# Graph attention on one Trainium2 core: both products of one late unit in sixteen from PSUM, two loads' room given to second sigmoids

## The chip, the cores and the metric

The kernel runs on one core of one Trainium2 chip. The metric is the device time of one execution in microseconds (us), lower is better.

## The reference

Two layers over N = 8192 nodes with 128 features, a dense 8192x8192 matrix `adj`, all in float32.

```python
# layer 0
A' = alpha * adj, with (1 - alpha) added on the diagonal
x1 = layernorm(x + relu((A' @ x / rowsum(A')) @ W.T + b))
# layer 1
t    = logmap0(x1)                               # a factor for each row
par  = adj   * sigmoid(t @ w_par[:d] [:, None] + t @ w_par[d:] [None, :] + b_par)
chi  = adj.T * sigmoid(t @ w_chi[:d] [:, None] + t @ w_chi[d:] [None, :] + b_chi)
out  = layernorm(x1 + proj(expmap0(chi @ t + par @ t)))
```

Almost all of the work of layer 1 is elementwise on 8192x8192: for each element two sigmoids, two products with `adj` or its transpose, and a product with the 128 columns of `t` on TensorE.

## The kernel before

The nodes are cut into 8 panels of 1024 rows. **Layer 0** goes over 256 pairs of tiles (`pair(g)`): SyncE loads 128x2048 values of `adj`, TensorE multiplies them with `x`, VectorE sums degrees. **Layer 1** is cut into 512 units. A unit n is one output panel p (1024 rows) against one tile jt of 128 columns, so 128x1024 elements, and it takes these steps:

- ScalarE (`sigmoids`, lines 707 to 738) computes the second sigmoid `chi(n)` (line 720) into an SBUF buffer and the first one (line 737) into a PSUM slot.
- GpSimd (`second_product`, lines 533 to 538) multiplies `chi(n)` in place with the untransposed tile ("nat", DRAM name in_a_cols).
- VectorE (`first_product`, line 986) multiplies the PSUM slot in place with the transposed tile ("trn", in_g_blk), and (`key`, line 995) adds `chi(n)` to it into one of three SBUF buffers `keys(n)`.
- TensorE (`products`, line 1180) multiplies `keys(n)` with the tile of `t` and sums into `outp`.

A unit of the set `APART` (line 268: n % 8 == 2 from unit 194, 35 units) has no `key`: VectorE writes its first product to `keys(n)`, and TensorE multiplies `keys(n)` and then `chi(n)` (line 1186), which adds the two in PSUM. Its buffer of `chi` is free only when TensorE has read it.

Units 0 to 153 are strewn into layer 0. Units 154 to 511 are the **late** ones, which come behind it. The late units go panel by panel: 64 units of one panel and, from 34 units on, 8 of an early one, so a period of the plan is 72 units. The last 8 of the 64 are the panel's **own** tiles (units 224 to 231, 296 to 303, 368 to 375, 440 to 447, 504 to 511), for which no transposed tile is loaded: TensorE transposes it from the nat tiles into the PSUM slot (`turn_own`, line 1196), two units ahead, and ScalarE writes the first sigmoid to SBUF. All 8 units of an own block need a part of all 4 nat loads, so these 4 entries come free only when the last transpose is done (line 469).

The order of everything is written out by hand and each engine works through its own list. What matters around the change:

- **Loads.** SyncE issues 1 MB loads (line 513), nat then trn for each two units, in order, into a ring of 7 entries in `ring` and from unit 160 on 3 more in `xA` (`RING`, `EXTRA`, lines 34 and 35). `wait_free` (line 454) waits until the entry's last user is through: `m2_ready`, counted by GpSimd's products, for nat, and `m1_ready`, by VectorE's first products, for trn.
- **Second sigmoids.** `buffer_of` (line 259) gives three buffers, and four from `MORE` = unit 184 on, where the fourth is a part of `xA`. ScalarE writes `chi(n)` when unit n-4 has been added (`k_ready`), or, where n-4 is in `APART`, multiplied by TensorE (`kt_used`). The last part of `xA` is a buffer for the own blocks (line 341).
- **PSUM slots.** `slot_plan` (line 144) hands out slots in turn, three from `SLOT_THREE` = unit 202 on. ScalarE's first sigmoid of unit n waits until the slot's last holder is done (`slot_free`, line 432). The norms of a finished panel (line 1205, 6 units into the next) and its transposed output (line 1215, 18 units in) each take a slot in the same rotation.
- **Finished panels.** In between, `evacuate` (760), the norms and their root (776, with a change of ScalarE's activation table), GpSimd's small steps, `add_residual` (1014), statistics (1022) and `final_normalise` (793, one of eight parts before each of eight units) run for one panel 34 or 38 units after the last.

```python
if before in APART:
    act.wait_ge(kt_used, before + 1)
elif before is not None:
    act.wait_ge(k_ready, SUMS[before])
```

Of the kernel before, what the change touches and what calls it, by code (L numbers as in the profile page):

```python
# [13 lines left out]
BP = 1024  # L14
# [17 lines left out]
PAIRS = NPAN * PPP  # L32
EARLY = 3
RING = 7
EXTRA = 3
CB = 3
KB = 3
SB = 3
PE_LAG = 2
# [101 lines left out]
SLOT_TWO, SLOT_THREE = LATE0, LATE0 + 48  # L141


def slot_plan():

    plans = {"unit": {}, "norms": {}, "final": {}}
    holder = {0: ("layer 0", 0), 1: ("passage", 0), 2: None}
    starts = {b + F_NORMS_SLOT: ("norms", k) for k, (_, b) in enumerate(FINALS)}
    starts |= {b + F_SLOT: ("final", k) for k, (_, b) in enumerate(FINALS)}
    uses = []  # L150
    for n in range(UNITS):
        if n in starts:
            uses.append(starts[n] + (n,))
        uses.append(("unit", n, n))
    uses += [("norms", len(FINALS) - 1, UNITS), ("final", len(FINALS) - 1, UNITS)]
    last = 2
    for kind, i, n in uses:
        if n < SLOT_TWO:
            s = 2
        elif n < SLOT_THREE:  # L160
            s = 0 if last == 2 else 2
        else:
            s = (last + 1) % SB
        last = s
        plans[kind][i] = (s, holder[s])
        holder[s] = (kind, i)
    return plans["unit"], plans["norms"], plans["final"]


SLOT_OF_UNIT, SLOT_OF_NORMS, SLOT_OF_FINAL = slot_plan()  # L170


def load_plan():

    kinds = []
# [80 lines left out]
MORE = LATE0 + 30  # L256


def buffer_of(n, few):

    if n < MORE:
        return n % few, n - few if n >= few else None
    k = (n - MORE) % (few + 1)
    return (few, n - few - 1 if n > MORE else None) if k == 0 else ((MORE + k - 1) % few, n - few - 1)

APART = {n for n in range(MORE + 8, UNITS) if n % 8 == 2 and n not in OWN_AT}

SUMS = [n + 1 - sum(m in APART for m in range(n + 1)) for n in range(UNITS)]  # L270

# [6 lines left out]
def adj_resnorm_kernel(nc, x_g, xT, g_blk, a_blk, WT, b_row, alpha, w_par, b_par, w_chi, b_chi, out):  # L278
    with ExitStack() as ctx:
# [3 lines left out]
        def sem(name):  # L283
            return ctx.enter_context(nc.semaphore(name))
# [46 lines left out]

        def chi(n):

            b, _ = buffer_of(n, CB)
            return chi_few[:, b, :] if b < CB else xA[:, EXTRA * CH:EXTRA * CH + BP]

        def keys(n):
            return keys_few[:, n % KB, :]


        own_par = [taken[:, :], xA[:, EXTRA * CH + BP:EXTRA * CH + 2 * BP]]

        def natural_of_own(n, k):

# [2 lines left out]
        def loaded(kind, j):  # L347

            e, c = LOAD_OF[(kind, j)]
            return entry(e), r_in[e], 16 * c  # L350
# [57 lines left out]
        m1_ready = sem("m1_ready")  # L408
        m2_ready = sem("m2_ready")
        k_ready = sem("k_ready")  # L410
        kt_used = sem("kt_used")
        out_evac = sem("out_evac")
        acc_added = sem("acc_added")
# [19 lines left out]
        def slot_free(eng, before):  # L433

            kind, i = before
            if kind == "unit" and i in APART:
                eng.wait_ge(m1_ready, i + 1)
            elif kind == "unit":
                eng.wait_ge(k_ready, SUMS[i])
            elif kind == "norms":  # L440
                eng.wait_ge(f_norm, i + 1)
            elif kind == "final":
                eng.wait_ge(v_ready, i + 1)
            elif kind == "layer 0":
                eng.wait_ge(y_evac, NPAN)
            else:
                eng.wait_ge(rows_ready, NPAN)
                eng.wait_ge(prcr_ready, NPAN)
# [3 lines left out]
        @block.sync  # L452
        def _(sp):
            def wait_free(e, before):
                if before is None:
                    if e >= RING:
                        sp.wait_ge(l0_used, PAIRS)
                    return
                kind, j = before
                if kind == "pair":  # L460

                    sp.wait_ge(l0_used, j + 1)
                    sp.wait_ge(deg_added, j + 2 if j % PPP == 0 else j + 1)
                elif kind == "trn":
                    sp.wait_ge(m1_ready, 2 * j + 2)
                else:
                    sp.wait_ge(m2_ready, 2 * j + 2)
                    if 2 * j in OWN_AT:
                        sp.wait_ge(own_turned, (OWN_AT[2 * j] // TPP + 1) * TPP)

            def load_x1(k):
                p, _ = FINALS[k]
                if k < 2:
                    sp.wait_ge(x1_out, 16 * NPAN)
                    sp.wait_ge(xt_ready, NPAN)
# [12 lines left out]

            for kind, j, e, before, _ in LOADS:
                if kind == "pair":  # L490
                    r, q = divmod(j, PPP)
                    if r == 0 and q % 2 == 0:
                        G = q // 2
                        src = x_g[G].rearrange("(a t) (c s d) -> s a c t d", t=2, s=2, d=D)
                        for h in range(2):
                            for c in range(2):
                                at = G * GC + c * 2 * D
                                sp.dma_start(xA[h * P // 2:(h + 1) * P // 2, at:at + 2 * D]
                                             .rearrange("a (t d) -> a t d", t=2), src[h, :, c]).then_inc(x_in[G], 16)
# [12 lines left out]
                wait_free(e, before)  # L512
                sp.dma_start(entry(e), src.rearrange("(p t) c -> p (t c)", t=2)).then_inc(r_in[e], 16)
            load_x1(NPAN - 1)
            store(NPAN - 2)
            store(NPAN - 1)
            sp.wait_ge(out_done, 16 * NPAN)

        @block.gpsimd
        def _(pool):  # L520
# [10 lines left out]
                                   op=ALU.add).then_inc(folded, 1)  # L531

            def second_product(n):
                t, here, count = loaded("nat", n // 2)
                pool.wait_ge(here, count)
                pool.wait_ge(c_ready, n + 1)
                pool.tensor_tensor(out=chi(n), in0=chi(n), in1=half(t, n),  # L537
                                   op=ALU.mult).then_inc(m2_ready, 1)
# [74 lines left out]
        def _(act):  # L613
# [93 lines left out]
            def sigmoids(n):  # L707
# [1 line left out]
                row, c, _ = rows_of(n)  # L709
                act.wait_ge(l_in[row], 32 * c)  # L710
                act.wait_ge(prcr_ready, jt // TPP + 1)
                b, before = buffer_of(n, CB)
                if before in APART:
                    act.wait_ge(kt_used, before + 1)
                elif before is not None:
                    act.wait_ge(k_ready, SUMS[before])
                elif b == CB:
                    act.wait_ge(l0_used, PAIRS)
                    act.wait_ge(res_ready, NPAN)
                act.activation(chi(n), scores[:, row, 1, :], ACT.Sigmoid,  # L720
                               bias=prcr[:, 2 * jt + 1:2 * jt + 2]).then_inc(c_ready, 1)
                if n in OWN_AT:
                    i = OWN_AT[n]
# [140 lines left out]
        def _(dve):  # L864
# [109 lines left out]
            def first_product(n):  # L974
# [10 lines left out]
                    dve.wait_ge(kt_used, n - KB + 1)  # L985
                dve.tensor_tensor(out=keys(n) if n in APART else s, in0=s, in1=other, op=ALU.mult).then_inc(m1_ready, 1)  # L986

            def key(n):
                if n in APART:
                    return  # L990
                dve.wait_ge(m1_ready, n + 1)
                dve.wait_ge(m2_ready, n + 1)
                if n >= KB:
                    dve.wait_ge(kt_used, n - KB + 1)
                dve.tensor_tensor(out=keys(n), in0=slots[SLOT_OF_UNIT[n][0]], in1=chi(n),  # L995
# [80 lines left out]
            for n in range(N_EARLY, UNITS):  # L1076
# [3 lines left out]
                    final(k, n - b)  # L1080
                if n == N_EARLY and PAIRS - 1 in UNIT_AT:
                    key(n - 1)
                first_product(n)
                key(n)
            k = NPAN - 1
# [9 lines left out]
        def _(pe):  # L1095
# [65 lines left out]
            def products(n):  # L1161
# [19 lines left out]
                                    keys(n)[:, h * BANK:(h + 1) * BANK], start=begins,  # L1181
                                    stop=is_end(n) and n not in APART)
                if n in APART:
                    pe.wait_ge(m2_ready, n + 1)
                    for h in range(BP // BANK):
                        ins = pe.matmul(outp[:, h * BANK:(h + 1) * BANK], xtA[:, jt * D:(jt + 1) * D],  # L1186
                                        chi(n)[:, h * BANK:(h + 1) * BANK], start=False, stop=is_end(n))
# [86 lines left out]
```

## Time and profile before

| | |
|---|---|
| Time, median of 3 runs | 2234.77 us (2233.01 to 2239.25) |
| Time of the profiled execution | 2237.35 us |
| Its span, first to last instruction | 2235.5 us |
| TensorE busy | 2039.8 us (91%) |
| VectorE busy | 1935.9 us (87%) |
| ScalarE busy | 1326.9 us (59%) |
| GpSimd busy | 1334.1 us (60%) |
| Moved by DMA | 818.29 MB, mean 366 GB/s |
| Mean granted TensorE clock | 0.976 |

The shares are means over two very different parts: layer 0 up to about 1255 us, in which ScalarE and GpSimd do little, and the late units from there to about 2212 us. Names in the profile: `ps` is a PSUM slot or `outp`, `chi` and `xA` the buffers of second sigmoids (`xA` also ring entries), `ring` the loads, in_a_cols a nat load and in_g_blk a trn load. PE is TensorE, DVE VectorE, ACT ScalarE, POOL GpSimd, SP SyncE. DMA landing times and waits are as the profile infers them from semaphores.

### The profile page before, as it was taken

The page shows a single profiled execution, that of the slowest core. Times are in us where ns is not written, and L with a number is a line of the kernel's source. Part 1 is how long each engine was busy: PE and PEld are TensorE (multiplying, and loading weights), DVE is VectorE, ACT ScalarE, POOL GpSimd, SP SyncE. Part 2 cuts the span into 40 slices and gives each one's busy share as a digit, 9 for nine tenths or more (in the row PEclk, how much of TensorE's full clock was granted, in tenths as well). Part 3 has the DMA queues.
Part 4 walks back from the last instruction along what each step waited for, and adds up shares of the span by engine and source line. Part 5 has one row for each costly group of instructions (what it writes and reads, how often), then busy time and mean ns, then how long its engine had stood idle before and what let it go on. Part 6 is the DMA issues. An engine that isn't in the chain of part 4 may idle for free. (4 is left out here: it accounts for less than half of the span.)

```text
span 2235.5 us, 18654 instructions
## 1 busy us (share of the span) xinstructions
PE 2039.8 (91%) x5240; PEld 919.1 (41%) x5240; DVE 1935.9 (87%) x1854; ACT 1326.9 (59%) x1512; POOL 1334.1 (60%) x607
## 2 busy tenths in 40 slices
PE   8999999999999999999999976998888889889886
PEld 3344444444444434444444432343344334334334
DVE  4676878988989988998998988898998998989996
ACT  0011324454454454453453587889888989999996
POOL 0000305435455555643543676999998998999995
PEclk9999999999999999999999988999999999999998
DMA  9998989899889988888888998999999999998992
GB/s 313 333 343 300 387 299 365 361 366 381 361 347 403 405 344 358 347 357 338 369 356 316 421 421 317 384 363 421 421 393 403 421 420 376 421 421 347 421 421 97
DMA packets 129207, 818.29 MB, mean 366 GB/s; under 512 B 14912, under 2 KB 27456, under 8 KB 33360
## 3 DMA queue, kind: packets, MB, share of 16 engines
q1 hardware_dynamic: 122304, 796.97, 89.1%
q10 hardware_dynamic: 6800, 20.13, 2.5%
q8 instruction: 43, 0.70, 0.1%
q14 instruction: 60, 0.49, 0.1%
HBM read 808.59 MB, written 8.45 MB: 365 GB/s over the span
## 5 line engine op out<-in xcount | busy, mean ns | idle before, releaser
L537 POOL TENSOR_TENSOR chi<-chi,ring 128x1024 f32<-128x1024 f32 x323 | 826.9, 2573 | 662.7 <-ACT chi L720 603.5
L1180 PE MATMUL ps<-keys,xtA 128*128 128x512 f32 x2048 | 986.4, 615 | 135.4 <-DVE keys L995 106.1
L1108 PE MATMUL ps<-ring,xA 128*128 128x512 f32 x2048 | 922.5, 600 | 37.9 <-DMA ring<-in_g_blk 33.6
L737 ACT ACTIVATE ps<-scores,prcr 128x1024 f32<-128x1024 f32 x472 | 521.9, 1106 | 389.5 <-DVE keys L995 379.2
L1180 PEld LDWEIGHTS ps<-keys,xtA 128*128 128x128 f32 x2048 | 382.3, 195 | 668.1 <-issue 629.0
L888 DVE TENSOR_TENSOR dsum<-dsum,ring 128x2048 f32<-128x2048 f32 x240 | 593.2, 2472 | 44.7 <-DMA ring<-in_g_blk 37.4
L1108 PEld LDWEIGHTS ps<-ring,xA 128*128 128x128 f32 x2048 | 386.5, 192 | 533.3 <-issue 468.8
L995 DVE TENSOR_TENSOR keys<-ps,chi 128x1024 f32<-128x1024 f32 x395 | 483.7, 1224 | 78.2 <-issue 29.2
L986 DVE TENSOR_TENSOR ps<-ps,ring 128x1024 f32<-128x1024 f32 x381 | 465.9, 1223 | 74.2 <-ACT ps L737 71.1
L720 ACT ACTIVATE chi<-scores,prcr 128x1024 f32<-128x1024 f32 x430 | 488.7, 1137 | 61.0 <-PE ps L1186 45.8
L537 POOL TENSOR_TENSOR chi<-chi,xA 128x1024 f32<-128x1024 f32 x107 | 251.9, 2372 | 32.4 <-ACT chi L720 32.3
L537 POOL TENSOR_TENSOR xA<-xA,ring 128x1024 f32<-128x1024 f32 x49 | 116.2, 2372 | 1.6 <-ACT xA L720 1.6
L995 DVE TENSOR_TENSOR keys<-ps,xA 128x1024 f32<-128x1024 f32 x82 | 100.4, 1225 | 6.6 <-DVE ps L986 2.4
L986 DVE TENSOR_TENSOR ps<-ps,xA 128x1024 f32<-128x1024 f32 x76 | 93.0, 1224 | 14.4 <-ACT ps L737 12.9
L530 POOL TENSOR_TENSOR dsum<-dsum 128x1024 f32<-128x1024 f32 x8 | 18.8, 2354 | 139.6 <-DVE dsum L888 137.2
L720 ACT ACTIVATE xA<-scores,prcr 128x1024 f32<-128x1024 f32 x82 | 93.0, 1134 | 0.4 <-ACT yb L671 0.4
L630 ACT ACTIVATE small<-mv,epsc 128x8 f32<-128x8 f32 x8 | 2.4, 301 | 150.6 <-DVE mv L922 150.6
L537 POOL TENSOR_TENSOR xA<-xA 128x1024 f32<-128x1024 f32 x33 | 78.3, 2374 | 5.0 <-ACT xA L720 5.0
L1186 PE MATMUL ps<-chi,xtA 128*128 128x512 f32 x140 | 65.8, 592 | 0.0
L884 DVE TENSOR_TENSOR dsum<-ring 128x1024 f32<-128x1024 f32 x16 | 34.3, 2182 | 31.8 <-PE ps L1117 17.4
L546 POOL TENSOR_TENSOR acc<-taken,acc 128x1024 f32<-128x1024 f32 x15 | 37.4, 2490 | 31.0 <-ACT taken L753 31.0
L720 ACT ACT_TABLE_LOAD x28 | 35.9, 1283 | 26.8 <-DVE prcr L954 22.6
(109 smaller groups left out, 818.6 us busy)
## 6 DMA issues: line engine op xcount, KB each, us to landing
ring<-in_g_blk SPq DMA_DIRECT2D x461, 1024.0 KB, 10.0
ring<-in_a_cols SPq DMA_DIRECT2D x186, 1024.0 KB, 9.9
xA<-in_a_cols SPq DMA_DIRECT2D x70, 1024.0 KB, 10.9
xA<-in_g_blk SPq DMA_DIRECT2D x31, 1024.0 KB, 12.6
scores<-plcl_d ACTq DMA_DIRECT2D x22, 512.0 KB, 8.1
xA<-in_x_g SPq DMA_DIRECT2D x64, 64.0 KB, 13.4
yb<-in_xT ACTq DMA_DIRECT2D x8, 512.0 KB, 8.8
x_d<-res ACTq DMA_DIRECT2D x8, 512.0 KB, 8.5
```

The source lines that it names most:

```text
L530: pool.tensor_tensor(out=dsum[:, 0:BP], in0=dsum[:, 0:BP], in1=dsum[:, BP:2 * BP], op=ALU.add).then_inc(folded, 1)
L537: pool.tensor_tensor(out=chi(n), in0=chi(n), in1=half(t, n), op=ALU.mult).then_inc(m2_ready, 1)
L546: pool.tensor_tensor(out=at, in0=taken[:, :], in1=at, op=ALU.add).then_inc(acc_added, 1)
L720: act.activation(chi(n), scores[:, row, 1, :], ACT.Sigmoid, bias=prcr[:, 2 * jt + 1:2 * jt + 2]).then_inc(c_ready, 1)
L737: act.activation(dst, scores[:, row, 0, :], ACT.Sigmoid, bias=prcr[:, 2 * jt:2 * jt + 1]).then_inc(p_ready, 1)
L884: dve.tensor_tensor(out=half(dsum, h), in0=half(t0, h), in1=half(t, h), op=ALU.add) \
L888: dve.tensor_tensor(out=dsum[:, :], in0=dsum[:, :], in1=t, op=ALU.add).then_inc(deg_added, 1)
L986: dve.tensor_tensor(out=keys(n) if n in APART else s, in0=s, in1=other, op=ALU.mult).then_inc(m1_ready, 1)
L995: dve.tensor_tensor(out=keys(n), in0=slots[SLOT_OF_UNIT[n][0]], in1=chi(n), op=ALU.add).then_inc(k_ready, 1)
L1108: ins = pe.matmul(Y[:, h * BANK:(h + 1) * BANK], xA[:, tile * D:(tile + 1) * D], t[:, tt * BP + h * BANK:tt * BP + (h + 1) * BANK], start= ...
L1180: ins = pe.matmul(outp[:, h * BANK:(h + 1) * BANK], xtA[:, jt * D:(jt + 1) * D], keys(n)[:, h * BANK:(h + 1) * BANK], start=begins, stop=i ...
L1186: ins = pe.matmul(outp[:, h * BANK:(h + 1) * BANK], xtA[:, jt * D:(jt + 1) * D], chi(n)[:, h * BANK:(h + 1) * BANK], start=False, stop=is_ ...
```

## The change

Seventeen late units, those with n % 16 == 6 from 214 on outside own blocks (214, 246, 262, ... 358, 390, ... 502), form a new set `DIRECT`, which is also added to `APART` (35 units become 52). In such a unit ScalarE writes both sigmoids to PSUM, each to a slot of its own ("second" just before "unit" in the rotation). GpSimd has no product. VectorE makes the second product (`second_of_direct`, PSUM slot times nat tile, into the SBUF buffer `chi(n)`) and then the first one into `keys(n)`, and it adds nothing. TensorE multiplies both. A new semaphore `d_ready` counts VectorE's second products, and where `m2_ready` was counted by units it is now counted by GpSimd's units alone (`BY_POOL`).

`EXTRA` goes from 3 to 2, so the ring has 9 entries in the late part where it had 10. The room in `xA` goes to `CB_MORE` = 3 buffers of second sigmoids where it was one: six in turn from unit 184 on, and ScalarE's write to `chi(n)` waits for unit n-6. The own blocks' buffer keeps its place at the end of `xA`.

The diff, cut to its core (in this order: constants, buffers, sets, slot plan, SyncE's `wait_free`, GpSimd, ScalarE's `sigmoids`, VectorE, TensorE's `products`):

```diff
-EXTRA = 3
+EXTRA = 2
 CB = 3
+CB_MORE = 3
...
-def buffer_of(n, few):
+def chi_buffer(n):
     if n < MORE:
-        return n % few, n - few if n >= few else None
-    k = (n - MORE) % (few + 1)
-    return (few, n - few - 1 if n > MORE else None) if k == 0 else ((MORE + k - 1) % few, n - few - 1)
+        return n % CB, n - CB if n >= CB else None
+    k = (n - MORE) % (CB + CB_MORE)
+    before = n - CB - CB_MORE
+    return (CB + k, before if before >= MORE else None) if k < CB_MORE else ((MORE + k - CB_MORE) % CB, before)
...
+DIRECT = {n for n in range(SLOT_THREE + 8, UNITS) if n % 16 == 6 and n not in OWN_AT}
+APART |= DIRECT
+BY_POOL = [n + 1 - sum(m in DIRECT for m in range(n + 1)) for n in range(UNITS)]
+BY_DVE = [sum(m in DIRECT for m in range(n + 1)) for n in range(UNITS)]
...
+        if n in DIRECT:
+            uses.append(("second", n, n))
         uses.append(("unit", n, n))
...
-                    sp.wait_ge(m2_ready, 2 * j + 2)
+                    sp.wait_ge(m2_ready, BY_POOL[2 * j + 1])
+                    if 2 * j in DIRECT or 2 * j + 1 in DIRECT:
+                        sp.wait_ge(d_ready, BY_DVE[2 * j + 1])
...
             def second_product(n):
+                if n in DIRECT:
+                    return
...
-                b, before = buffer_of(n, CB)
-                if before in APART:
+                b, before = chi_buffer(n)
+                if n in DIRECT:
+                    s, held = SLOT_OF_SECOND[n]
+                    slot_free(act, held)
+                elif before in APART:
                     act.wait_ge(kt_used, before + 1)
...
-                act.activation(chi(n), scores[:, row, 1, :], ACT.Sigmoid,
+                act.activation(slots[s] if n in DIRECT else chi(n), scores[:, row, 1, :], ACT.Sigmoid,
...
+            def second_of_direct(n):
+                if n not in DIRECT:
+                    return
+                t, here, count = loaded("nat", n // 2)
+                dve.wait_ge(here, count)
+                dve.wait_ge(c_ready, n + 1)
+                _, before = chi_buffer(n)
+                if before in APART:
+                    dve.wait_ge(kt_used, before + 1)
+                else:
+                    dve.wait_ge(k_ready, SUMS[before])
+                dve.tensor_tensor(out=chi(n), in0=slots[SLOT_OF_SECOND[n][0]], in1=half(t, n),
+                                  op=ALU.mult).then_inc(d_ready, 1)
...
+                second_of_direct(n)
                 first_product(n)
                 key(n)
...
-                    pe.wait_ge(m2_ready, n + 1)
+                    if n in DIRECT:
+                        pe.wait_ge(d_ready, BY_DVE[n])
+                    else:
+                        pe.wait_ge(m2_ready, BY_POOL[n])
```

## Rows read from the trace of the kernel before

**Rows 1.** Windows: length; busy PE, PEld, DVE, ACT, POOL (instructions); clock; DMA share; GB/s.
```profile
1420.00:1475.00 55.00, 48.22 (x109) 19.68 (x109) 51.27 (x44) 50.30 (x49) 54.94 (x24) 0.97 0.98 397
1475.00:1512.00 37.00, 35.89 (x136) 20.27 (x135) 34.60 (x30) 32.58 (x32) 34.65 (x16) 1.00 0.85 333
1709.40:1894.60 185.20, 163.17 (x436) 73.74 (x436) 169.94 (x191) 167.70 (x175) 171.37 (x89) 0.98 0.99 407
...
1420.00:2215.00 795.00, 700.67 (x1885) 315.95 (x1884) 730.55 (x779) 714.52 (x730) 739.02 (x368) 0.99 0.95 391
```

**Rows 2.** Chain that ended last, over the whole run: start us, us, what.
```profile
...
1709.41 7.12 PE ps L1180 x12
1716.53 1.73 PE ps L1186 x4
...
1894.64 7.11 PE ps L1180 x12
...
```

**Rows 3.** Chain that ended last, from 1894 to 2080 us.
```profile
by line: POOL chi L537 28.9%; issue 18.5%; PE ps L1180 16.2%; POOL xA L537 8.9%; ACT chi L720 5.3%; ACT ps L737 4.2%; PE ps L1196 4.1%; DVE keys L995 2.7%; ACT xA L720 2.3%; PE ps L1186 1.9%; DVE ps L986 1.4%; DVE res L1014 1.0%; ACT L720 0
...
2047.39 1.72 PE ps L1180 x4
2049.11 0.95 PE ps L1196 x8
```

**Rows 4.** Waits of VectorE, 1420 to 2212 us: us in total, times, longest.
```profile
DVE ps L986 <- ACT ps L737: 22.2, 16, 3.2
DVE keys L995 <- POOL chi L537: 16.3, 25, 1.5
```

**Rows 5.** Waits of ScalarE, the same stretch.
```profile
ACT chi L720 <- PE ps L1186: 43.7, 25, 2.4
ACT ps L737 <- DVE keys L995: 6.6, 14, 1.6
```

**Rows 6.** Waits of GpSimd, the same stretch.
```profile
POOL chi L537 <- ACT chi L720: 43.2, 35, 2.8
```

**Rows 7.** Groups of instructions by form, 1300 us to the end.
```profile
L537 POOL TENSOR_TENSOR chi<-chi,ring 128x1024 f32<-128x1024 f32 x163 | 384.2, 2377 | 43.0 <-ACT chi L720 42.8
L737 ACT ACTIVATE ps<-scores,prcr 128x1024 f32<-128x1024 f32 x307 | 338.1, 1101 | 22.4 <-DVE keys L995 14.8 <-DVE res L1014 5.4 <-DVE yb L1014 1.6
L720 ACT ACTIVATE chi<-scores,prcr 128x1024 f32<-128x1024 f32 x264 | 300.0, 1136 | 46.4 <-PE ps L1186 45.8 <-DVE keys L995 0.5
L995 DVE TENSOR_TENSOR keys<-ps,chi 128x1024 f32<-128x1024 f32 x231 | 282.9, 1225 | 39.0 <-POOL chi L537 18.8 <-DVE ps L986 7.7 <-issue 3.8
...
L986 DVE TENSOR_TENSOR keys<-ps,ring 128x1024 f32<-128x1024 f32 x29 | 35.2, 1214 | 0.4 <-ACT ps L737 0.4
```

**Rows 8.** Timeline around the norms of one panel (line 776), 1966 to 1976 us.
```profile
1968.34 1.28 ACT L776 ACT_TABLE_LOAD   x1
...
1970.02 1.28 ACT L720 ACT_TABLE_LOAD   x1
...
1972.37 1.10 ACT L737 ACTIVATE ps<-scores,prcr 128x1024 f32<-128x1024 f32 x1
...
1973.57 1.23 DVE L986 TENSOR_TENSOR ps<-ps,ring 128x1024 f32<-128x1024 f32 x1 [1.70 <-ACT ps L737]
```

**Rows 9.** Waits of SyncE's DMA queue in one period, 1709 to 1895 us.
```profile
SPq L469 <- PE ps L1196: 17.6, 1, 17.6
```

**Rows 10.** DMA in the same period: 40 slices, sums, one group of issues.
```profile
GB/s 425 423 421 423 418 419 423 423 421 423 409 426 425 423 421 423 423 423 417 424 423 421 416 421 421 419 421 423 412 428 426 423 74 227 403 421 426 425 421 418
DMA packets 11684, 75.80 MB, mean 408 GB/s; under 512 B 1217, under 2 KB 2241, under 8 KB 2885
...
xA<-in_a_cols SPq DMA_DIRECT2D x15, 1024.0 KB, 11.1
```

**Rows 11.** Timeline of one load and the product that reads it.
```profile
1724.51 0.33 SPq L513 DMA_DIRECT2D xA<-in_a_cols  x1
...
1744.06 2.37 POOL L537 TENSOR_TENSOR xA<-xA 128x1024 f32<-128x1024 f32 x1
```

More of the change, by code:

```diff
@@ L141 @@
 SLOT_TWO, SLOT_THREE = LATE0, LATE0 + 48
[L144 to L170, printed above, removed]
 def load_plan():
@@ L256, with slot_plan @@
 MORE = LATE0 + 30
-def buffer_of(n, few):
+def chi_buffer(n):
     if n < MORE:
-        return n % few, n - few if n >= few else None
-    k = (n - MORE) % (few + 1)
-    return (few, n - few - 1 if n > MORE else None) if k == 0 else ((MORE + k - 1) % few, n - few - 1)
+        return n % CB, n - CB if n >= CB else None
+    k = (n - MORE) % (CB + CB_MORE)
+    before = n - CB - CB_MORE
+    return (CB + k, before if before >= MORE else None) if k < CB_MORE else ((MORE + k - CB_MORE) % CB, before)
 APART = {n for n in range(MORE + 8, UNITS) if n % 8 == 2 and n not in OWN_AT}
+DIRECT = {n for n in range(SLOT_THREE + 8, UNITS) if n % 16 == 6 and n not in OWN_AT}
+APART |= DIRECT
+BY_POOL = [n + 1 - sum(m in DIRECT for m in range(n + 1)) for n in range(UNITS)]
+BY_DVE = [sum(m in DIRECT for m in range(n + 1)) for n in range(UNITS)]
 SUMS = [n + 1 - sum(m in APART for m in range(n + 1)) for n in range(UNITS)]
+def slot_plan():
+    plans = {"unit": {}, "second": {}, "norms": {}, "final": {}}
+    holder = {0: ("layer 0", 0), 1: ("passage", 0), 2: None}
+    starts = {b + F_NORMS_SLOT: ("norms", k) for k, (_, b) in enumerate(FINALS)}
+    starts |= {b + F_SLOT: ("final", k) for k, (_, b) in enumerate(FINALS)}
+    uses = []
+    for n in range(UNITS):
+        if n in starts:
+            uses.append(starts[n] + (n,))
+        if n in DIRECT:
+            uses.append(("second", n, n))
+        uses.append(("unit", n, n))
+    uses += [("norms", len(FINALS) - 1, UNITS), ("final", len(FINALS) - 1, UNITS)]
+    last = 2
+    for kind, i, n in uses:
+        if n < SLOT_TWO:
+            s = 2
+        elif n < SLOT_THREE:
+            s = 0 if last == 2 else 2
+        else:
+            s = (last + 1) % SB
+        last = s
+        plans[kind][i] = (s, holder[s])
+        holder[s] = (kind, i)
+    return plans["unit"], plans["second"], plans["norms"], plans["final"]
+SLOT_OF_UNIT, SLOT_OF_SECOND, SLOT_OF_NORMS, SLOT_OF_FINAL = slot_plan()
 LAST_OF_EARLY = {ENDS[k]: k for k, (p, _, a) in enumerate(GROUPS) if p < EARLY and a == NPAN - 1}
@@ L332, in chi @@
         def chi(n):
-            b, _ = buffer_of(n, CB)
-            return chi_few[:, b, :] if b < CB else xA[:, EXTRA * CH:EXTRA * CH + BP]
+            b, _ = chi_buffer(n)
+            at = EXTRA * CH + (b - CB) * BP
+            return chi_few[:, b, :] if b < CB else xA[:, at:at + BP]
         def keys(n):
             return keys_few[:, n % KB, :]
-        own_par = [taken[:, :], xA[:, EXTRA * CH + BP:EXTRA * CH + 2 * BP]]
+        own_par = [taken[:, :], xA[:, EXTRA * CH + CB_MORE * BP:EXTRA * CH + (CB_MORE + 1) * BP]]
         def natural_of_own(n, k):
@@ L410, in adj_resnorm_kernel @@
         k_ready = sem("k_ready")
+        d_ready = sem("d_ready")
         kt_used = sem("kt_used")
@@ L439, in slot_free @@
                 eng.wait_ge(k_ready, SUMS[i])
+            elif kind == "second":
+                eng.wait_ge(d_ready, BY_DVE[i])
             elif kind == "norms":
@@ L716, in sigmoids @@
                     act.wait_ge(k_ready, SUMS[before])
-                elif b == CB:
+                elif b >= CB:
                     act.wait_ge(l0_used, PAIRS)
                     act.wait_ge(res_ready, NPAN)
-                act.activation(chi(n), scores[:, row, 1, :], ACT.Sigmoid,
+                act.activation(slots[s] if n in DIRECT else chi(n), scores[:, row, 1, :], ACT.Sigmoid,
                                bias=prcr[:, 2 * jt + 1:2 * jt + 2]).then_inc(c_ready, 1)
@@ L991, in key @@
                 dve.wait_ge(m1_ready, n + 1)
-                dve.wait_ge(m2_ready, n + 1)
+                dve.wait_ge(m2_ready, BY_POOL[n])
                 if n >= KB:
@@ L1183, in products @@
                 if n in APART:
-                    pe.wait_ge(m2_ready, n + 1)
+                    if n in DIRECT:
+                        pe.wait_ge(d_ready, BY_DVE[n])
+                    else:
+                        pe.wait_ge(m2_ready, BY_POOL[n])
                     for h in range(BP // BANK):
```

## The prediction

> **What bounds the kernel now.** I read the windows first, then the chain, the waits of each engine, the forms, and the DMA last. Everything that the change touches lies behind unit 202, which starts at about 1420 us. From there to 2215 us the busy times of the four compute engines are nearly level: GpSimd 739.0, VectorE 730.6, ScalarE 714.5 and TensorE 700.7 of 795 us, and DMA is at 0.95 [rows 1]. So no single engine's total is the bound; the time goes where one of them makes the next wait. One stretch is the exception: from 1420 to 1475 us GpSimd is busy 54.94 of 55 us with VectorE at 51.27 [rows 1].
>
> The plan's period of 72 units is seen in the chain, which comes back to the same place 1894.64 - 1709.41 = 185.2 us later, 2.57 us per unit [rows 2]. Within a period GpSimd's products hold 28.9 + 8.9 = 38% of the chain and TensorE some 22%, the latter mostly in the own blocks, where a unit costs it 1.72 us of products beside 0.95 us of transposes [rows 3], the last of eight such pairs. VectorE, which has the most to hand on, waits 22.2 us in all for ScalarE's first sigmoids and 16.3 us for GpSimd's products [rows 4]. The source of many of these is one step up: ScalarE waits 43.7 us, 25 times, for TensorE's product with `chi` of an APART unit (line 1186), so 1.75 us each, before it may write the second sigmoid of unit n+4 [rows 5], and GpSimd then waits 43.2 us for ScalarE [rows 6]. The chain shows it too: 1.73 us of line 1186 follow on 7.12 us of line 1180 [rows 2], and what comes next there is the second sigmoid.
>
> **The change part by part.**
>
> (A) GpSimd loses 17 products of 2.377 us [rows 7], 40.4 us of its 739.0, four or five in a period. They are on the path only where VectorE waited for GpSimd: 16.3 us in 25 waits [rows 4]. Bounds: nothing, if those waits move to another releaser, and 16.3 us. I take two thirds, 11 us, since a skipped product puts GpSimd 2.4 us ahead for the units after it and no wait is longer than 1.5 us, but 17 skips do not stand before all 25 waits.
>
> (B) Six buffers of second sigmoids. ScalarE's write waits for unit n-6, two units earlier, so two periods of 2.57 us, and no wait of rows 5 is longer than 2.4 us: they go, all 43.7 us, the new APART units' among them. ScalarE cannot use more than that, since its first sigmoid still needs a slot that VectorE lets go three units back. What reaches VectorE are its 22.2 us of waits for ScalarE [rows 4]. Some of these have another cause: with each panel's norms ScalarE loads its table twice, 1.28 us each, and VectorE then waits 1.70 us [rows 8]; seven times, that is 12 us and stays. The other 10 us I take as gone. Bounds: 0 and 22.2 us.
>
> (C) VectorE has two instructions in a DIRECT unit as in an ordinary one: the second product in place of the sum, 1.214 us (nearest row: PSUM and ring in, SBUF out) for 1.225 us [rows 7]. Over 17 units that is nothing. ScalarE writes to PSUM in 1.101 us where it wrote to SBUF in 1.136 [rows 7], 0.6 us over all, nothing as well. What counts is the order. The unit takes two of three slots, so its first sigmoid waits for the sum of unit n-2, where it waited for n-3. Counted from the sum of n-3: second sigmoid done at 1.1, first at 2.45 + 1.1 = 3.55, the next unit's second at 4.7, its first, which waits for the sum of n-1 at 4.9, at 6.0. VectorE makes the unit's products from 4.9 to 7.3 and needs the latter only then: 1.3 us to spare. Queued behind ScalarE's wait are its later sigmoids, and one part of a finished panel's normalisation fits in the 1.3 us. So I take nothing for 15 of the units. Two of them, 310 and 454, stand where the norms also take a slot and the tables are loaded; there no slack is left (1.70 us of waiting already [rows 8]), and the wait for one more unit costs 2 x 1.22 = 2.4 us each: +4.9 us. Bounds for the whole: 0, and 17 x 2.45 = 42 us if every DIRECT unit loses a full unit of ScalarE's lead. I stay near the lower end, as ScalarE's present waits for slots are 6.6 us in 14, 0.47 us each [rows 5].
>
> (D) TensorE gets 17 x 1.73 us [rows 2] more, 29 us on 700.7; it has 94 us of idle time there [rows 1]. This cover is missing in and just before the own blocks, where it runs without a gap. Units 294 and 438 stand one unit before an own block: 2 x 1.7 = 3.4 us. Bounds 0 and 29 us.
>
> (E) The ring of 9. Each load is 1.049 MB, 2.49 us at 421 GB/s. A load issued at 1724.51 takes a median 11.1 us [rows 10] and its first reader starts at 1744.06 [rows 11]: it lies ready for 8.5 us. With one entry fewer it is issued later, but while DMA is saturated the issue time only shortens the queue. The own block is different: SyncE stands 17.6 us at line 469 [rows 9] and DMA runs dry, two slices of 4.65 us at 74 and 227 GB/s [rows 10], 6.0 us of lost transfer. With 9 entries one load less is ahead of that point, so all loads of the period land 2.5 us later and 6.0 of the 8.5 us stay. Cost 0 now; above, 4 x 2.5 = 10 us if the margin is used up; a gain is excluded, since fewer loads are ahead. In a DIRECT unit the nat entry is also let go by VectorE rather than GpSimd; GpSimd's product of its neighbour in the same load is about as late, and what is queued on SyncE behind it has the same margin. On GpSimd's queue nothing new waits.
>
> The sum: -11 - 10 + 4.9 + 3.4 = -12.7 us. The profiled execution took 2237.35 us (span 2235.5) and would take 2224.6; it lies 2.6 us above the median, 2234.77, from which the forecast is 2222 us, -0.6%. For this kernel about 0.3%, 7 us, is what a measurement can tell from no change.
>
> The DMA floor deserves a weighing. The row says that the loads run at 421 to 425 GB/s through a period, with 75.80 MB in 186 us [rows 10]: 180 us of transfer, so a period can't go under some 179 us in 185.2. The Trainium skill (DMA: Bandwidth & Descriptors, "Where 436 GB/s comes from") puts 435 GB/s for the ports into SBUF and says that for HBM to SBUF about 358 GB/s binds. By the second figure the kernel's 818 MB would take 2286 us, more than the whole run, and the change could bring nothing; this case's rows contradict it for one core alone, and they stand close under the first.
>
> **The rivals.**
>
> *Nearly all waits go.* A and B bring 16.3 + 22.2 us and C and D nothing. For it: the waits are short and the lead grows. Then DMA is the bound: a period loses its 6.0 us of dry time and no more, four periods 24 us, and with the saving of one product in the stretch bound by GpSimd, 2.4 us, the time is 2208 us. Against: 9 entries give back up to 2.5 us of each 6.0. 0.17.
>
> *Waits change their names.* ScalarE's 43.7 us turn into waits for slots, GpSimd idles 40 us more, and VectorE, busy 92% and with small gaps between any two instructions, sets the pace, with TensorE in the own blocks. For it: the level busy times [rows 1]. A and B then bring about the 8 us that C and D cost, or little more: 2229 to 2236, at 2233 us. 0.22.
>
> *Slower by the slots.* The pair of slots drains ScalarE's lead at each DIRECT unit. Place: the first sigmoid (line 737) of the unit and of the one after. Price: up to 2.45 us each, 42 us, less 21 from A and B, plus 3.4: at full 2259, at half 2238. It decides once a DIRECT unit costs VectorE over (21 - 3.4)/17 = 1.0 us in the mean. For it: one slot fewer for a unit, and ScalarE is loaded 90% [rows 1]; against: the 1.3 us of slack. 0.16 for a loss above 0.3%, at 2248 us.
>
> **How the numbers follow.** The forecast has 0.45, with a range of its own of 2212 to 2229 us. The range for 8 in 10 reaches to the DMA floor on one side and into the slots' case on the other: 2207 to 2242. Faster by over 0.3% (under 2228): 0.41 of the forecast's, 0.17 of the first rival and a little of the second, 0.60. Within 0.3%: 0.23. Slower by over 0.3%: 0.17.
>
> **What would show it.** Right: ScalarE's waits for line 1186 near zero; VectorE's waits for GpSimd under 6 us; its waits for ScalarE near 15, with those at units 310 and 454 over 3 us; GpSimd busy 699 us behind 1420; the period 182 us; a dry time of DMA of some 5 us in an own block; no wait of VectorE or GpSimd for DMA. It is wrong if VectorE's new product takes over 1.3 us or slows GpSimd's over 2.4, if first products behind DIRECT units wait over 1 us for line 737 each time (slots), if waits for in_g_blk or in_a_cols appear in mid-panel (ring), or if the period stays at 185 us with fewer named waits.

## The result and the profile after

| | before | after |
|---|---|---|
| Time, median of 7 runs each | 2234.77 us (2228.63 to 2241.34) | 2256.24 us (2249.84 to 2258.92) |
| Ratio | 1 | 1.0089, 95% interval 1.0075 to 1.0104 |
| Span of the profiled execution | 2235.5 us | 2255.7 us |

The change makes the kernel 0.9% slower, 20 us. The forecast was 2222 us, with a range of 2207 to 2242 us. What the ring gave up is one entry, the room of one load of 1 MB, which holds two buffers of second sigmoids of half that size; "two loads' room" in the title says too much.

First the late part by window, with the columns of [rows 1], for the kernel after:

```profile
1420.00:2235.00 815.00, 728.02 (x1952) 332.21 (x1952) 730.12 (x779) 715.75 (x729) 700.81 (x351) 0.98 0.93 382
```

The work came out as the diff says: GpSimd fell from 739.0 to 700.8 us, TensorE rose from 700.7 to 728.0, VectorE and ScalarE are where they were. DMA was busy 0.95 of the time and is at 0.93. No engine but TensorE has more work, and TensorE keeps 87 us of idle time, so the loss is mostly waiting. Here are the waits of the four engines, taken over the late part of the kernel after (1420 to 2232 us; us in total, times, longest), beside [rows 4 to 6]:

```profile
POOL xA L555 <- ACT xA L741: 60.1, 28, 6.8
...
POOL chi L555 <- ACT chi L741: 47.0, 43, 5.2
ACT ps L758 <- DVE keys L1030: 32.2, 56, 2.1
DVE ps L1007 <- ACT ps L758: 26.4, 15, 4.3
DVE ps L1007 <- PE ps L1235: 25.9, 40, 4.0
...
ACT xA L758 <- DVE ps L1007: 18.1, 15, 3.9
ACT taken L758 <- DVE ps L1007: 16.2, 15, 4.1
...
PE ps L1235 <- DMA ring<-in_a_cols: 10.0, 6, 3.3
...
DVE keys L1030 <- POOL chi L555: 7.0, 15, 1.1
...
DVE keys L1030 <- POOL xA L555: 5.9, 9, 1.1
...
PE ps L1235 <- DMA xA<-in_a_cols: 5.4, 2, 3.0
```

Lines have moved: 1007 is VectorE's first product (986 before), 741 and 758 ScalarE's second and first sigmoids, 555 GpSimd's product, 1216 and 1225 TensorE's products, and 1235 the transposes of an own block. ScalarE's 43.7 us of waits for TensorE's product with `chi` are gone, and 32.2 us of waits for a slot stand in their place (6.6 before). New in size are the waits at the transposes: TensorE waits 15.4 us there for loads, and VectorE 25.9 us, 40 times, for TensorE; five blocks of eight units are 40. In the kernel before (1420 to 2212 us) the same waits were short:

```profile
DVE ps L986 <- PE ps L1196: 2.1, 12, 0.2
...
PE ps L1196 <- DMA ring<-in_a_cols: 1.8, 1, 1.8
...
PE ps L1196 <- DMA xA<-in_a_cols: 1.0, 1, 1.0
```

The chain that ended last, which in this kernel reaches back to the start of the run, says the same. These are the last of its pieces (start us, us, what) in a list of the 60 longest, each just before an own block:

```profile
1464.19 11.90 DMA ring<-in_a_cols
...
1649.51 15.85 DMA xA<-in_a_cols
...
1843.99 12.51 DMA ring<-in_a_cols
...
2030.50 12.49 DMA xA<-in_a_cols
...
2197.66 11.34 DMA ring<-in_a_cols
```

All five own blocks hang on a load. In the kernel before, the chain reaches back only to 1702 us, so only to the last three own blocks, and it passes through a load at two of these three, at 1832.50 and 2176.85 us. So the loads already held the kernel before at some blocks, by less.

The second own block shows how it goes, in the timeline of the kernel after (start us, us, engine, line, what, in brackets the idle time before and what ended it):

```profile
1657.38 1.19 DVE L1020 TENSOR_TENSOR xA<-ps,ring 128x1024 f32<-128x1024 f32 x1
...
1658.49 1.21 DVE L1007 TENSOR_TENSOR keys<-ps,ring 128x1024 f32<-128x1024 f32 x1
...
1658.85 0.85 PE L1235 MATMUL ps<-ident,ring 128*128 128x128 f32 x4
...
1661.66 0.70 PE L1235 MATMUL ps<-ident,ring 128*128 128x128 f32 x2 [1.96 <-DMA ring<-in_a_cols]
...
1665.41 0.70 PE L1235 MATMUL ps<-ident,xA 128*128 128x128 f32 x2 [3.04 <-DMA xA<-in_a_cols]
...
1665.90 3.21 PE L1216 MATMUL ps<-keys,xtA 128*128 128x512 f32 x4
1666.15 1.23 DVE L1007 TENSOR_TENSOR ps<-ps,taken 128x1024 f32<-128x1024 f32 x1 [4.05 <-PE ps L1235]
...
1668.94 1.88 PE L1225 MATMUL ps<-xA,xtA 128*128 128x512 f32 x4
...
1670.66 0.88 PE L1235 MATMUL ps<-ident,ring 128*128 128x128 f32 x6
...
1671.82 1.23 DVE L1007 TENSOR_TENSOR ps<-ps,xA 128x1024 f32<-128x1024 f32 x1 [3.17 <-PE ps L1235]
```

At 1658.85 TensorE begins the eight transposes of unit 296, two units ahead. They need all four nat loads of the block; TensorE gets at the third at 1661.7 us and at the fourth at 1665.4, and VectorE stands still for 4.05 us. Then TensorE has unit 294 to catch up, a DIRECT unit with the product of line 1225 on top, before it may transpose for unit 297: 3.17 us more. Before, the same place cost TensorE one wait of 1.81 us, and VectorE, still busy with the units ahead, nothing:

```profile
1660.47 0.51 PE L1196 MATMUL ps<-ident,ring 128*128 128x128 f32 x2 [1.81 <-DMA ring<-in_a_cols]
...
1660.82 1.88 PE L1180 MATMUL ps<-keys,xtA 128*128 128x512 f32 x4
1661.10 1.22 DVE L986 TENSOR_TENSOR ps<-ps,taken 128x1024 f32<-128x1024 f32 x1
```

TensorE's granted clock fell there too. The windows around the waits, with the columns of [rows 1], first of the kernel after, then of the kernel before:

```profile
1656.00:1661.70 5.70, 3.47 (x11) 1.42 (x9) 5.67 (x13) 5.30 (x6) 4.79 (x3) 1.00 1.03 412
1661.70:1668.50 6.80, 3.76 (x8) 1.82 (x9) 2.72 (x3) 2.68 (x4) 4.55 (x2) 0.50 1.01 425
```

```profile
1661.70:1668.50 6.80, 6.80 (x33) 4.42 (x32) 6.42 (x6) 5.44 (x6) 6.80 (x4) 1.00 1.01 420
```

0.50 is 1.2 of 2.4 GHz. Behind the wait of 1.96 us TensorE runs at half its clock for 6.8 us, with the next wait of 3.04 us inside, and the four products at 1665.90 take 3.21 us where four take 1.88 at the full clock. In this trace the clock is at 0.5 for 17 us in four of the five own blocks, and in none of them in the trace of before. A late load so costs its wait and then a slower TensorE.

Last, the DMA of one period after, 1718 to 1905 us, in 40 slices of 4.7 us:

```profile
GB/s 414 423 419 422 417 424 424 421 417 424 422 410 431 422 421 421 422 421 419 415 422 421 421 422 421 424 421 426 408 431 428 354 11 96 368 426 426 422 421 421
```

The slices of 354, 11, 96 and 368 GB/s lack (67 + 410 + 325 + 53)/421 of a slice, 9.5 us of transfer; counted so, with its 403 too, [rows 10] lacked 6.2 us. SyncE's wait at the own block (line 485) is 22.3 us, 17.6 before [rows 9].

### The profile page after: what moved, and what is told of

Same layout as the page of the kernel before. It is cut to its first block, busy times and chain, and to the rows that moved or that the text cites. A ratio compares the mean times of both kernels' runs of the same rounds, so it can differ in the third digit from the quotient of the medians.

```text
span 2255.7 us, 18774 instructions
## 1 busy us (share of the span) xinstructions
PE 2068.2 (92%) x5308; PEld 937.3 (42%) x5308; DVE 1936.6 (86%) x1854; ACT 1329.3 (59%) x1512; POOL 1296.6 (57%) x590
## 4 chain that ended last, share of the span: by engine, by line
PE 40%; POOL 18%; DVE 13%; issue 12%; ACT 9%; DMA 7%; DVEq 0%; ACTq 0%; SPq 0%; POOLq 0%
PE ps L1144 24%; POOL chi L555 11%; PE ps L1216 11%; POOL xA L555 6%; DVE dsum L909 4%; DMA ring<-in_g_blk 4%; DVE ps L1007 3%; ACT chi L741 2%; PE ps L1235 2%; DVE keys L1030 2%; DMA ring<-in_a_cols 2%; ACT ps L758 2%; DMA xA<-in_a_cols 1%; ACT xA L741 1%; ACT L741 1%
## 5 line engine op out<-in xcount | busy, mean ns | idle before, releaser
L555 POOL TENSOR_TENSOR chi<-chi,ring 128x1024 f32<-128x1024 f32 x294 | 759.0, 2593 | 666.2 <-ACT chi L741 606.6
L1007 DVE TENSOR_TENSOR ps<-ps,ring 128x1024 f32<-128x1024 f32 x360 | 440.1, 1223 | 81.7 <-ACT ps L758 79.9
L1030 DVE TENSOR_TENSOR keys<-ps,chi 128x1024 f32<-128x1024 f32 x330 | 404.0, 1224 | 65.7 <-issue 30.7
L741 ACT ACTIVATE chi<-scores,prcr 128x1024 f32<-128x1024 f32 x343 | 389.5, 1136 | 15.5 <-DMA scores<-plcl_d 8.4
L555 POOL TENSOR_TENSOR xA<-xA,ring 128x1024 f32<-128x1024 f32 x127 | 299.0, 2374 | 58.2 <-ACT xA L741 57.4
L741 ACT ACTIVATE xA<-scores,prcr 128x1024 f32<-128x1024 f32 x152 | 172.4, 1134 | 0.0
L1030 DVE TENSOR_TENSOR keys<-ps,xA 128x1024 f32<-128x1024 f32 x130 | 159.2, 1225 | 13.6 <-POOL xA L555 6.1
L555 POOL TENSOR_TENSOR chi<-chi,xA 128x1024 f32<-128x1024 f32 x49 | 115.7, 2376 | 18.2 <-ACT chi L741 18.1
L1007 DVE TENSOR_TENSOR ps<-ps,xA 128x1024 f32<-128x1024 f32 x80 | 97.9, 1224 | 22.6 <-PE ps L1235 14.5
L555 POOL TENSOR_TENSOR xA<-xA 128x1024 f32<-128x1024 f32 x25 | 59.1, 2375 | 14.9 <-ACT xA L741 14.6
L1225 PE MATMUL ps<-xA,xtA 128*128 128x512 f32 x140 | 66.4, 597 | 0.0
## 6 DMA issues: line engine op xcount, KB each, us to landing
xA<-in_x_g SPq DMA_DIRECT2D x64, 64.0 KB, 13.3
```

Source lines behind the costliest of these rows:

```text
L555: pool.tensor_tensor(out=chi(n), in0=chi(n), in1=half(t, n), op=ALU.mult).then_inc(m2_ready, 1)
L741: act.activation(slots[s] if n in DIRECT else chi(n), scores[:, row, 1, :], ACT.Sigmoid, bias=prcr[:, 2 * jt + 1:2 * jt + 2]).then_inc(c_r ...
```

## The experiments

Three theories stood after the traces: **R**, the entry taken from the ring makes the loads of own blocks late; **S**, a DIRECT unit's second slot costs at each such unit; **D**, a DIRECT unit's product on TensorE costs where an own block follows. Ratios are to the kernel before, run on the same chip, with 95% intervals.

**DIRECT units on the old ring.**

```diff
-EXTRA = 2
+EXTRA = 3
-CB_MORE = 3
+CB_MORE = 1
```

> The changed kernel's DIRECT units with the ring of 10 entries and four buffers of second sigmoids, as before the change (EXTRA 3, CB_MORE 1). Theory R (the loss comes from the ring: the four nat loads of an own block land after TensorE wants to transpose them): nothing of the loss is left, 2225 to 2236 us, and TensorE waits under 4 us in all for in_a_cols at the transposes. Theory S (the loss comes from the slots that a DIRECT unit takes): the whole loss stays, 2250 to 2258 us. Theory D (TensorE's extra products before the own blocks): 2240 to 2246 us, with VectorE waiting 3 us for the second transpose of the blocks behind units 294 and 438 alone.

Measured: 2242.82 us, 1.0029 (1.0018 to 1.0041). A third of the loss is there with the old ring, so R alone isn't enough, and S does not carry the whole. The time lies in the range of D.

**Six buffers and the ring of 9, no DIRECT units.**

```diff
-DIRECT = {n for n in range(SLOT_THREE + 8, UNITS) if n % 16 == 6 and n not in OWN_AT}
+DIRECT = set()
```

> The changed kernel without DIRECT units (the set is empty), so six buffers of second sigmoids and a ring of 9 alone. Theory R: the loss is there, 2245 to 2258 us, and TensorE waits 10 to 20 us in all for in_a_cols at the transposes of own blocks. Theories S and D: no loss, 2220 to 2236 us. In any case ScalarE's 43.7 us of waits for the product of chi are gone.

Measured: 2248.47 us, 1.0055 (1.0039 to 1.0071). R holds: neither S nor D has a place in this kernel. TensorE waits 12.4 us for loads at the transposes. Its waits from 1420 to 2240 us:

```profile
ACT ps L758 <- DVE keys L1030: 26.7, 53, 2.6
...
DVE ps L1007 <- ACT ps L758: 18.5, 11, 3.7
DVE ps L1007 <- PE ps L1235: 15.4, 30, 3.4
...
PE ps L1235 <- DMA ring<-in_a_cols: 8.4, 6, 3.3
...
PE ps L1235 <- DMA xA<-in_a_cols: 4.0, 2, 3.2
```

Here too ScalarE's wait has only changed its name, from TensorE's product to the slot, and of VectorE's 22.2 us for ScalarE [rows 4] only 3.7 are gone.

**The ring of 9 alone.**

```diff
-DIRECT = {n for n in range(SLOT_THREE + 8, UNITS) if n % 16 == 6 and n not in OWN_AT}
+DIRECT = set()
-CB_MORE = 3
+CB_MORE = 1
```

> Only the ring goes from 10 to 9 entries: no DIRECT units, four buffers of second sigmoids, the freed room unused. Theory R: 2248 to 2260 us, at or above the changed kernel, since nothing pays for the lost entry. Theories S and D: 2232 to 2238 us, the time of before. It gives the price of one entry of the ring by itself.

Measured: 2247.25 us, 1.0049 (1.0033 to 1.0065). This is just under R's range, which began at 2248 us, and below the changed kernel, where R had put it at or above: the ring alone is not the whole loss. One entry of the ring is worth 11 us. The two extra buffers bring nothing that a measurement can tell: 1.0055 with them, 1.0049 without.

**DIRECT units, the ring of 9, four buffers.**

```diff
-CB_MORE = 3
+CB_MORE = 1
```

> DIRECT units and the ring of 9, but four buffers of second sigmoids (the freed room unused). Beside the changed kernel (2256 us) it gives what six buffers bring on a ring of 9. If the six buffers are worth what ScalarE's waits of before suggest: 2262 to 2275 us. If ScalarE was ahead anyway and only waits elsewhere: 2252 to 2260 us.

Measured: 2253.69 us, 1.0073 (1.0057 to 1.0088), beside 1.0089 for the changed kernel. Again six buffers bring nothing that can be told; the intervals overlap. The shares add up: 0.49% for the ring and 0.29% for DIRECT are 0.78%.

**Where in the run.** From the traces I took the end of VectorE's first product of some units and subtracted that of the kernel before and the difference at unit 204 (which comes from ahead of the change, -4.4 to 4.5 us in these traces), in us. Each row is a single execution:

```
unit                  222   234   292   306   366   378   436   450   500   511
own block before it         224         296         368         440         504
ring of 9 alone      -0.0   1.2   1.1   4.5   4.5   7.0   7.0   7.0   6.9  11.9
six buffers, ring 9  -0.1   0.9   0.7   4.1   3.4   6.8   6.0   6.7   5.4  11.7
DIRECT, ring of 10   -0.3  -0.3  -1.7   2.5   2.0   2.7   0.7   2.3   4.6   5.0
inner DIRECT, r. 10  -0.3  -0.3  -1.7   0.9   1.0   1.2  -0.7  -0.7   1.5   0.3
edge DIRECT, r. 10   -0.0  -0.0  -0.1   1.5   1.3   1.5   0.8   2.4   2.4   4.2
after                -0.9   4.0   2.1   9.2   8.7  13.4  10.9  16.6  17.7  20.9
```

The ring of 9 alone loses only across own blocks (1.2, 3.4, 2.5, 0.0 and 5.0 us) and between them no more than 0.1 us either way. ("Inner" and "edge" are two kernels that follow.) Six buffers gain 0.2 to 1.3 us in a panel and give it back at the next block. The changed kernel gains 1.9, 0.5 and 2.5 us in three panels, loses 1.1 in the last, and pays 4.9, 7.1, 4.7, 5.7 and 3.2 us at the blocks. The price of one block varies from execution to execution: the changed kernel without units 294, 438 and 502, which is the same program up to unit 292, paid 1.4 us at the first block where this trace has 4.9. There TensorE had waited 0.9 us for loads and kept its clock, here it waited 2.6 us and had the clock at 0.5 for 3.4 us.

The loss of a block has three parts in the traces. One is the part of the wait that reaches VectorE. Another is the pace behind it: once TensorE has no lead, VectorE takes 2.67 us a unit instead of 2.40, up to 1.9 us in the seven units that are left; at the block of unit 368 the ring of 9 alone loses 0.7 us and then 0.27 a unit, 2.5 in all. The third is the clock. In the 14 traces of this study it fell 16 times in an own block, each time around a wait of 2.0 to 3.3 us for a load; some waits of 2 to 3.3 us passed without a fall, and in no own block without such a wait did it fall. Its price can be estimated at the first block, some 1.5 us: with waits of 2.6 us and the low clock it cost 4.9 us (after), with waits of 2.4 us and the full clock 3.2 us (the changed kernel with relieved loads, below).

**DIRECT units without those just before an own block.** D says that units 294 and 438, and 502 as well, all two before an own block, are what costs.

```diff
-... if n % 16 == 6 and n not in OWN_AT}
+... if n % 16 == 6 and n not in OWN_AT and n + 2 not in OWN_AT}
```

> Ring of 10 and four buffers of second sigmoids as before the change, with DIRECT units except 294, 438 and 502, which stand two units before an own block (14 are left). Theory D (what DIRECT units cost by themselves is TensorE's extra product at the door of an own block): 2228 to 2233 us, under before, with VectorE's waits for the transposes near the 2.1 us of before and not 8.2. Theory S (the slots cost, everywhere): the loss shrinks only with the count, 14/17 of 0.3%, 2239 to 2242 us.

Measured: 2236.54 us, 1.0004 (0.9996 to 1.0013). 0.25% of the 0.29% hung on three units of 17. What is left is neither the gain that I expected nor a cost: 14 fewer products on GpSimd are worth nothing here. In the trace it is a balance: 1.4 and 1.9 us gained in two panels, 2.6 lost at the block of unit 296 behind a late load and 2.2 in the panel of unit 454, 1.2 won back at the last block. VectorE waits 14.5 + 1.9 us for GpSimd, 18.2 before, and 25.7 us for ScalarE, 22.2 before; its waits at the transposes are 4.2 us, where D expected some 2.1.

**Only the three units just before an own block**, the complement (n + 2 in OWN_AT), on the ring of 10.

> Ring of 10, four buffers of second sigmoids, and as DIRECT units only the three that stand two units before an own block (294, 438, 502). Theory D: they carry the whole cost of the 17, so 2239 to 2244 us, with VectorE waiting some 3 us at the second transposes of those blocks. If the cost of the 17 is spread: 2234 to 2238 us.

Measured: 2240.38 us, 1.0023 (1.0014 to 1.0032), so D holds: 5.1 us for three units, as much as TensorE's work for them, 3 x 1.7 us. In the trace the blocks behind them lose 1.6, 1.6 and 1.8 us, with the full clock. VectorE's wait at the second transpose was less than expected, 1.80 us in the block behind unit 294:

```profile
1662.33 1.23 DVE L1007 TENSOR_TENSOR ps<-ps,xA 128x1024 f32<-128x1024 f32 x1 [1.80 <-PE ps L1235]
...
1665.00 1.23 DVE L1007 TENSOR_TENSOR ps<-ps,taken 128x1024 f32<-128x1024 f32 x1 [0.17 <-PE ps L1235]
```

From there VectorE goes at TensorE's pace, 1665.00 - 1662.33 = 2.67 us a unit, where before it took 2.40 to 2.67.

**The changed kernel without the three units.** The same edit, with the ring of 9 and six buffers.

> The changed kernel without the DIRECT units 294, 438 and 502: ring of 9, six buffers. If the shares add up (ring with six buffers +0.55%, inner DIRECT units +0.04%): 2247 to 2250 us. If the doors of own blocks lose on a late load whatever else they do, so that the three units cost nothing more there: 2253 to 2257 us.

Measured: 2249.57 us, 1.0064 (1.0049 to 1.0078): the shares add up on the short ring as well.

**Relief for DMA.** If the loads' time is what costs, shorter loads should give the loss back though the ring stays at 9. In three kernels 40 of the late loads bring half of their data, with every wait left as it is; the kernel leaves out a part of the matrix:

```diff
+                if kind != "pair" and 2 * j in HALVED:
+                    sp.dma_start(entry(e)[:, 0:BP], src.rearrange("(p t) c -> p t c", t=2)[:, 0, :]).then_inc(r_in[e], 16)
+                else:
...
+HALVED = {i - back for i in OWN[::TPP] if i > N_EARLY for back in (24, 20, 16, 12)}
```

> The kernel before with DMA relieved: in each panel 8 of the late loads (those of units 24, 20, 16 and 12 before each own block) bring only half of their data, 40 half loads in all, 10 us of transfer in each panel; the rest of those tiles keeps old values, so part of the matrix is left out. Theory R says that before was nearly free of waits for loads (2.8 us in all): 2231 to 2236 us. If the loads already held the kernel before in a way the waits do not name: under 2225 us.

> Six buffers of second sigmoids and the ring of 9, no DIRECT units, with the same 40 half loads (part of the matrix is left out). Theory R: the whole loss of 0.5% of this kernel with full loads is lateness of the own block's loads, so it goes, and what the six buffers bring in mid-panel stays: 2226 to 2234 us, and TensorE's waits for loads at the transposes are under 3 us instead of 12.4. If the ring hurts in another way (entries let go late, not transfer time): 2243 to 2250 us.

> The changed kernel with the same 40 half loads (part of the matrix is left out). Theory R plus D: the ring's share of the loss goes and the share of the DIRECT units at the door of own blocks stays, 2234 to 2244 us. If all of the loss is lateness of loads: 2222 to 2233 us. If it is slots: 2250 us or more.

| | full loads | 40 half loads |
|---|---|---|
| before | 1 | 0.9980 (0.9970 to 0.9989) |
| six buffers, ring of 9 | 1.0055 | 0.9971 (0.9959 to 0.9984) |
| after | 1.0089 | 0.9995 (0.9984 to 1.0006) |

The relief brings 4.5 us to the kernel before, 19 us to six buffers on 9 entries and 21 us to the changed kernel. It takes away transfer time and no entry, so it is the landing times that cost, not the count of entries by itself. In the half-loaded six-buffer kernel TensorE waits 0.8 us for loads at the transposes, and in no own block of the three traces does its clock fall. The kernel before gained more than its own waits for loads (2.8 us) let one see: it too was held by the loads at 296 and at 504 (the shift above falls by 1.8 and 1.3 us there). Behind the relief the changed kernel is still 0.15% slower than the relieved kernel before. The blocks behind the three units lose 1.6, 1.6 and 1.8 us against it, as they did alone, and the first block 3.2; some of this is won back between blocks. Six buffers may bring something once loads are no limit, 0.9971 beside 0.9980, but the intervals overlap.

**The transposes one unit ahead instead of two**, which lets the block ask for its loads 2.5 us later, on the ring of 9 and on the ring of 10:

```diff
-                if n + 2 in OWN_AT:
-                    turn_own(n + 2)
+                if n + 1 in OWN_AT:
+                    turn_own(n + 1)
```

> The ring of 9 alone (2247 us), with the transposes of own tiles one unit ahead instead of two, so that the first of a block asks for its four loads 2.5 us later. Theory R: the waits for loads at the transposes fall from 7.7 us to under 2 us; what TensorE's shorter lead costs at 8 units of each block is not known: 2238 to 2246 us if it is small, up to 2256 us if it is not.

> The kernel before with the transposes one unit ahead instead of two: it gives the price of the shorter lead by itself, with waits for loads of only 2.8 us to win. If the lead is worth nothing beside those waits: 2231 to 2235 us, a version faster than both kernels. If VectorE then waits for TensorE at each own unit (2.67 against 2.40 us a unit, five blocks): 2240 to 2247 us.

Measured: 2248.97 us, 1.0059 (1.0045 to 1.0073) on 9 entries, and 2250.13 us, 1.0058 (1.0042 to 1.0073) on 10, above both ranges that were expected for it. With the later request the entry is worth nothing that can be told, which fits a price that hangs on that request: waits for loads are 1.8 us on the ring of 9. But the second unit of lead is worth as much itself, 13 us: VectorE waits 13.3 us, 40 times, for the transposes in the second kernel.

No kernel of the study was faster than the kernel before with all its loads; the nearest, with 14 DIRECT units, is level with it.

## Why the prediction was wrong

**(E), the ring, is the step that failed.** It read: "Cost 0 now". It took a load that a GpSimd product uses, ready for 8.5 us, and gave this margin to all loads. The four nat loads of an own block have an earlier reader: TensorE's first transposes, two units ahead and for all four loads at once. The trace of before had it in view, as waits for in_a_cols at line 1196 of 2.8 us in all, and I read [rows 9] and [rows 10] for what happens behind the block and not for what waits at its entry. The margin there was nothing, and the waits then lowered the clock as well. The same step gave 2.5 us for one load less; at the blocks the ring alone cost 1.2, 3.4, 2.5, 0.0 and 5.0 us in its trace, and 11 us (0.49%) by the medians, close to the upper bound of 10 that I named and set aside. I counted four periods where there are five own blocks, and the last cost the most.

**(D)** had the place, the mechanism and the price of a unit right: 3.4 us for units 294 and 438. Unit 502 was forgotten, and the three cost 5.1 us alone and 5.6 us as the difference of 1.0029 and 1.0004. They stand two units before an own block, not one, which is where TensorE begins its transposes.

**(A)** was 11 us and is next to nothing. GpSimd lost 38 us of work and VectorE's waits for it fell from 18.2 (16.3 in [rows 4], 1.9 for `xA`) to 12.9 us in the changed kernel, but only to 16.4 with 14 DIRECT units on the old ring. Two thirds of the waits for GpSimd was no price, and neither was its share in the chain, 38% [rows 3]: with 14 units VectorE's waits for it fell by 1.8 us and those for ScalarE rose by 3.5.

**(B)**: the waits of [rows 5] went to the last, as forecast, and 10 us for the path was wrong. ScalarE came up against the slots instead, and 43.7 us of waiting turned into 32.2 us for `ps`; its first sigmoids kept VectorE waiting 26.4 us, not the 15 forecast. That was the rival "waits change their names", for this part. The traces put the gain at 0.2 to 1.3 us a panel, and the time on the ring of 9 shows none.

**(C)**, which led my slow rival, cost less than I took. The second product took 1.202 to 1.210 us (1.214 forecast), and the coincidence with the norms cost 2.0 us at unit 454 and 0.2 at 310, not 2.4 at each. With 14 units the whole of A and C is a loss of 0.04%, within the noise. The rival that ended slower had the sign right and the cause wrong.

With what the runs showed for each term, the sum is about 1 (A and C, 0.04%) + 1 (B, the difference of 1.0055 and 1.0049) + 11 (E) + 5.1 to 5.6 (D), some 18 us; 20 were measured, 17 to 23 by the interval, so nothing clear of the noise is left over. The forecast had -12.7. Of the 33 us between it and the result, 21 are the gains of A and B that did not come and 11 the ring that was taken as free: with E right alone the sum would have been -2 us, level with before, and with A and B right alone 8 us.

**The DMA floor** was read right but put on the wrong side. I saw that a period cannot go under some 179 us of transfer and used it as a cap on a gain. It also means that little of what is won between blocks survives, as the rows of the table show: the next block waits for a landing time that DMA sets. The transfer rate stayed at 421 GB/s, and 435 GB/s for the ports, which the Trainium skill gives (DMA: Bandwidth & Descriptors, "Where 436 GB/s comes from"), stays the figure near it.

## What to carry to other kernels

Price a prefetch buffer by the first reader that needs the load, and for a block that needs several loads at once by the last of them; look for the wait that already exists there, however short, since a wait of 2 us means a margin of nothing. Count with a late load more than its wait: behind it TensorE had lost its lead, and in 16 blocks its clock too. Where DMA is saturated, as here, work saved between two such points was mostly given back at the next one, and a buffer taken from the loads cost at four of five. Before engine work is moved to an engine with idle time in the mean, look whether it lands next to the stretch in which that engine sets the pace: three of 17 units carried 0.25 of the 0.29% that they cost.

## What the runs showed of the hardware

VectorE's product of a PSUM slot with an SBUF tile took 1.204 us into `xA` and 1.210 into `chi` beside GpSimd's products, which kept their 2.374 to 2.380 us (2.372 to 2.377 before). The Trainium skill (SBUF — State Buffer, "SBUF: two separate sides") says that a VectorE operation with both inputs in SBUF and a GpSimd operation that reads SBUF lock each other out, whichever starts first. With one input in PSUM, as here, GpSimd's products kept their time, which agrees; no run here puts the new product's two inputs in SBUF.

TensorE's granted clock fell from 1.00 to 0.50 in own blocks only around waits for loads of 2.0 to 3.3 us, for 3.4 or 6.8 us. Four 128x512 products then took 3.21 us in place of 1.88.
